# Queries and keys stacked side by side, three transfers a head, and a head's turn back one step sooner, in an attention and expert kernel

## What is computed

```python
q, k, v = (split_heads(x @ W + b) for W, b in ((Wq, bq), (Wk, bk), (Wv, bv)))
attn = q @ k.T / sqrt(32) - slopes * (Tx - 1 - arange(Tx))     # (4, 16, 512, 512)
p = softmax(where(causal, attn, min))
x = layernorm(x + (p @ v) @ Wo + bo)
probs = softmax(x @ Wr + br); top_w, e = top_k(probs, 1)
x = layernorm(x + top_w * (silu(x @ Wg[e]) * (x @ Wu[e])) @ Wd[e])
```

## Time and profile before

| what | us |
|---|---|
| median of 2 runs | 1335.26 (1333.82 to 1336.7) |
| the profiled execution | 1339.05 |
| its span (first to last instruction) | 1337.3 |
| PE busy | 1179.2 (88%) |
| DVE, ACT, POOL busy | 729.9, 592.3, 522.0 |
| first scores of the loop | at 29.2 |
| first products of the experts (L902) | at 614.4 |

### The profile page before, as it was taken

One profiled execution on the slowest core, in us unless ns is written; L12 is line 12 of the kernel. 1 busy time (PEld: TensorE's weight loads), 2 busy tenths in 40 slices (PEclk: granted clock), 3 DMA queues, 4 the chain that ended last, 5 costly groups with the idle time before them and its releaser, 6 DMA issues.

```text
span 1337.3 us, 25993 instructions
## 1 busy us (share of the span) xinstructions
PE 1179.2 (88%) x7658; PEld 1051.2 (79%) x7658; DVE 729.9 (55%) x1975; ACT 592.3 (44%) x1475; POOL 522.0 (39%) x662
## 2 busy tenths in 40 slices
PE   6867788888888887858999999999999999999994
PEld 5755676677667666647899889988999889998993
DVE  4544446544654456464655655465645664565565
ACT  3556666566566665723332323232322333233344
POOL 6744644454445454635311332133202331133136
PEclk9888988888888988767999999999999999999998
DMA  8222223222232222115322223231323122312302
GB/s 261 55 48 48 48 57 87 64 49 56 65 87 48 49 64 77 52 63 160 86 79 80 59 69 96 64 91 45 87 65 95 50 79 69 90 57 72 95 26 102
DMA packets 110336, 100.13 MB, mean 75 GB/s; under 512 B 13247, under 2 KB 82495, under 8 KB 110208
## 3 DMA queue, kind: packets, MB, share of 16 engines
q1 hardware_dynamic: 105440, 87.98, 23.8%
q0 software_dynamic: 3040, 9.18, 2.1%
q10 hardware_dynamic: 1728, 1.31, 0.3%
HBM read 64.74 MB, written 9.18 MB: 55 GB/s over the span
## 4 chain that ended last, share of the span: by engine, by line
PE 60%; SPq 9%; POOL 8%; DMA 7%; issue 6%; DVE 5%; ACT 5%; ACTq 0%; DVEq 0%; POOLq 0%
PE bank L902 33%; PE bank L674 9%; SPq L557 7%; POOL up_lo L1629 6%; PE bank L927 6%; DMA q_stack<-qk_lo 3%; PE bank L820 3%; DMA up_raw<-in_Wu_dram 3%; PE bank L914 2%; PE bank L780 2%; PE bank L795 2%; DVE bank L1283 1%; ACT up_hi L1057 1%; ACT qk_hi L983 1%; SPq L578 1%
## 5 line engine op out<-in xcount | busy, mean ns | idle before, releaser
L902 PE MATMUL bank<-up_hi,xsT_hi 128*128 x1216 | 356.2, 293 | 9.9 <-POOL up_lo L1629 9.4
L1629 POOL TENSOR_TENSOR up_lo<-up_raw,up_hi 128x256 fp32r<-128x256 f32 x241 | 171.7, 748 | 483.0 <-ACT up_hi L1057 482.8
L902 PE MATMUL bank<-up_hi,xsT_lo 128*128 x1216 | 344.6, 283 | 0.0
L902 PE MATMUL bank<-up_lo,xsT_hi 128*128 x1216 | 344.5, 283 | 0.0
L1620 POOL TENSOR_TENSOR pT_lo<-probs,pT_hi 128x512 fp32r<-128x512 f32 (+1 forms) x192 | 211.4, 1101 | 196.2 <-ACT pT_hi L1034 196.0
L1444 DVE SCALAR_TENSOR_TENSOR h_tok<-bank,row_weight,silu 128x128 f32<-128x128 f32 x304 | 93.4, 347 | 296.1 <-ACT silu L1138 296.1
L902 PEld LDWEIGHTS bank<-up_hi,xsT_hi 128*128 128x128 f32 x1216 | 233.3, 192 | 16.7 <-issue 16.4
L902 PEld LDWEIGHTS bank<-up_hi,xsT_lo 128*128 128x128 f32 x1216 | 234.0, 192 | 0.3
L902 PEld LDWEIGHTS bank<-up_lo,xsT_hi 128*128 128x128 f32 x1216 | 233.6, 192 | 0.0
L1138 ACT ACTIVATE silu<-bank 128x256 f32<-128x256 f32 (+1 forms) x160 | 59.9, 374 | 365.8 <-PE bank L902 365.8
L1461 DVE TENSOR_TENSOR y<-bank,y 128x512 f32<-128x512 f32 x295 | 199.0, 690 | 0.4
(11 more groups left out here) (181 smaller groups left out, 2145.5 us busy)
## 6 DMA issues: line engine op xcount, KB each, us to landing
up_raw<-in_Wg_dram SPq DMA_DIRECT2D x64, 256.0 KB, 3.5
up_raw<-in_Wu_dram SPq DMA_DIRECT2D x64, 256.0 KB, 4.5
down_raw<-in_Wd_dram SPq DMA_DIRECT2D x64, 256.0 KB, 2.6
k_stack<-qk_hi SPq DMA_DIRECT2D x128, 64.0 KB, 2.0
q_stack<-qk_hi SPq DMA_DIRECT2D x128, 64.0 KB, 2.0
x_tok<-in_x_dram SPq DMA_DIRECT2D x16, 256.0 KB, 3.8
k_stack<-qk_lo SPq DMA_DIRECT2D x64, 64.0 KB, 2.0
q_stack<-qk_lo SPq DMA_DIRECT2D x64, 64.0 KB, 2.0
```

The costliest lines, as they stand in the source:

```text
L902: mm = pe.matmul(bank[:, n * 2 * P:(n + 1) * 2 * P], a[:, s, k, :], up_w[w][k][:, :, :].rearrange("p a f -> p (a f)")[:, bass.ds(at, 2 * P ...
L1629: pool.tensor_tensor(up_w[1][k][:, e, :], up_raw[:, idx % NUPS, k, :, :].rearrange("p g f -> p (g f)"), up_w[0][k][:, e, :].bitcast(F32), ...
```

## The change

1. `qk_hi` and `qk_lo` become one buffer `qk` of four parts in the order low q, high q, high k, low k, and `q_stack` and `k_stack` become one buffer `stack` with both side by side in a slot. One transfer fills a third of the slot for both: three transfers a head with twice the bytes each (the first group keeps six a head, by `load_first_part`, since its keys are ready before its queries).
2. SP looks in every step, not only in every third, whether a head's stacks can be loaded.
3. On ACT the copy to `pvT` stands at the end of step s instead of early in step s+1; PE's turn stands in step s+1 instead of s+2; the copy of the high half, the sum and the division in step s+2 instead of s+3.
4. The plan takes the first job of its queue whose needs are met; rows' jobs are queued in other steps; V jobs of the first groups come later; K and Q of some groups come earlier in their group.

```diff
+LOW, HIGH = {WQ: 0, WK: 3}, {WQ: 1, WK: 2}
+STACKED = ((HIGH[WQ], HIGH[WK]), (LOW[WQ], HIGH[WK]), (HIGH[WQ], LOW[WK]))
...
-    row_steps = ((), (0, 1, 6), (0, 3), (2, 6)), ((), (0, 4), (0, 4), (0, 1, 5))
+    row_counts = (0, 3, 2, 2), (0, 2, 2, 3)
...
-                if any(k not in ready for k in needs(queue[0])):
+                now_job = next((j for j in queue if all(k in ready for k in needs(j))), None)
+                if now_job is None:
                     return
...
-                if m in (1, 2) and b < LAST:
+                if m == 2 and 0 < b < LAST:
                     queue.extend([("K", g + 1), ("Q", g + 1)])
...
-        if is_head_step(u, VL + PER_HEAD + 3):
-            ready.add(("o", (u - VL - PER_HEAD - 3) // PER_HEAD))
+        if is_head_step(u, VL + PER_HEAD + 2):
+            ready.add(("o", (u - VL - PER_HEAD - 2) // PER_HEAD))
...
-                for n in (WK, WQ):
-                    load_part(hd, n, False)
-                    load_part(hd, n, True)
+                for r, (q_part, k_part) in enumerate(STACKED):
+                    sp.dma_start(stack[r * HD:(r + 1) * HD, hd % NSTK, :, :].bitcast(F32),
+                                 qk[h * HD:(h + 1) * HD, q_part:k_part + 1:k_part - q_part, :].bitcast(F32)
+                                 ).then_inc(s_stack[hd % NSTK], 16)
...
                     load_row((u - ROW_AT) // PER_HEAD)
-                    for _ in range(2):
-                        if (next_stack < NB * NH and plan.flushed[("Q", next_stack // GH)] <= u
-                                and (next_stack < NSTK or (next_stack - NSTK) * PER_HEAD + PER_HEAD - 1 + LAG < u)):
-                            load_stacks(next_stack)
-                            next_stack += 1
+                for _ in range(2):
+                    if (next_stack < NB * NH and plan.flushed[("Q", next_stack // GH)] <= u
+                            and (next_stack < NSTK or (next_stack - NSTK) * PER_HEAD + PER_HEAD - 1 + LAG < u)):
+                        load_stacks(next_stack)
+                        next_stack += 1
...
-                if is_head_step(u, VL + PER_HEAD + 1):
-                    head_values((u - VL - PER_HEAD - 1) // PER_HEAD)
+                if is_head_step(u, VL + PER_HEAD):
+                    head_values((u - VL - PER_HEAD) // PER_HEAD)
...
-                if is_head_step(u, VL + PER_HEAD):
-                    head_copied((u - VL - PER_HEAD) // PER_HEAD)
-                if is_head_step(u, VL + PER_HEAD + 2):
-                    head_values((u - VL - PER_HEAD - 2) // PER_HEAD)
+                if is_head_step(u, VL + PER_HEAD + 1):
+                    head_values((u - VL - PER_HEAD - 1) // PER_HEAD)
                 if is_head_step(u, ROW_AT):
                     copy_row((u - ROW_AT) // PER_HEAD)
                 if LAG <= u < U + LAG:
                     unit_exp(u - LAG)
+                if is_head_step(u, VL + PER_HEAD - 1):
+                    head_copied((u - VL - PER_HEAD + 1) // PER_HEAD)
```

More of the change, by code:

```diff
@@ L165, in make_plan @@
         plan.flushed[job] = 0
-    ready = {("x", b, j) for b in range(2) for j in range(QT)} | {("read",) + job for job in first}
+    ready = {("begun", "OP", -1), ("begun", "logit", -1)} | {("x", b, j) for b in range(2) for j in range(QT)} | {("read",) + job for job in first}
     queue, left, now_job, pending, later = deque(), [], None, [], deque()
     rows_due, fresh = deque(), []
-    row_steps = ((), (0, 1, 6), (0, 3), (2, 6)), ((), (0, 4), (0, 4), (0, 1, 5))
+    row_counts = (0, 3, 2, 2), (0, 2, 2, 3)
     def needs(job):
@@ L178, in needs @@
         if kind == "OT":
-            return [("o", t // QT * NH + (DONE if t // QT == LAST else NH) - 1)]
-        return {"OP": [("read", "OT", t)], "x1t": [("ln", t)], "logit": [("read", "x1t", t)], "bv_wo": [("split", kind)]}[kind]
+            return [("o", t // QT * NH + (DONE if t // QT == LAST else NH) - 1), ("begun", "OP", t - 1)]
+        return {"OP": [("read", "OT", t)], "x1t": [("ln", t), ("begun", "logit", t - 1)], "logit": [("read", "x1t", t)], "bv_wo": [("split", kind)]}[kind]
     def flush(u):
@@ L202, in work @@
                     return
-                now_job = queue.popleft()
+                queue.remove(now_job)
+                ready.add(("begun",) + now_job)
                 plan.add(now_job, 2)
@@ L254, in make_plan @@
                 if g == 0:
-                    queue.extend([("K", 1), ("Q", 1), ("V", 1, 0), ("bv_wo", 0)])
+                    queue.extend([("K", 1), ("Q", 1), ("bv_wo", 0)])
                 elif m == 0:
                     queue.appendleft(("V", g // 2, 1))
-                elif m == 1:
-                    queue.append(("V", g // 2 + 1, 1))
-                elif m == GPB - 1 and b + 1 < NB:
+                    rows_due.extend((b - 1, n) for n in range(QT + 3))
+                elif g == 1:
+                    queue.append(("V", 1, 0))
+                elif m == 1 or g == 2:
+                    queue.appendleft(("V", b * GPB // 2 + 1, 1))
+                for _ in range(row_counts[b == LAST][m] if b else 0):
+                    queue.extend(row_jobs(*rows_due.popleft()))
+                if m == GPB - 1 and b + 1 < NB:
                     next_x = b + 1
                     queue.append(("V", (g + 1) // 2, 0))
-                if m == 0 and g:
-                    rows_due.extend((b - 1, n) for n in range(QT + 3))
             for j in range(QT):
@@ L391, in build @@
         xT_lo = p1.put("xT_lo", [P, KT, SEQ], F32R)
-        qk_hi = p1.put("qk_hi", [P, 2, SEQ], F32R)
-        qk_lo = p1.put("qk_lo", [P, 2, SEQ], F32R)
+        qk = p1.put("qk", [P, 4, SEQ], F32R)
         stacks_at = p1.at
-        k_stack = p1.put("k_stack", [3 * HD + 1, NSTK, SEQ], F32R)
-        q_stack = p1.put("q_stack", [3 * HD + 1, NSTK, SEQ], F32R)
+        stack = p1.put("stack", [3 * HD + 1, NSTK, 2, SEQ], F32R)
+        q_stack, k_stack = stack[:, :, 0, :], stack[:, :, 1, :]
         v = p1.put("v", [P, 2, QT, 2 * GH, VW], F32R)
@@ L548, in load_x, with load_first_part @@
                 sp.dma_start(x_tok[:, (b + 1) % 2, j, :], x_rows[b, :, j, :]).then_inc(s_x[b % 2][j], 16)
-            def load_part(hd, n, low):
-                h, slot = hd % GH, hd % NSTK
+            def load_first_part(h, n, low):
                 rows = slice(h * HD, (h + 1) * HD)
[L554 to L558, removed]
+                for r, (q_part, k_part) in enumerate(STACKED):
+                    part = k_part if n == WK else q_part
+                    if (part in LOW_PARTS) == low:
+                        sp.dma_start(stack[r * HD:(r + 1) * HD, h, 1 if n == WK else 0, :].bitcast(F32),
+                                     qk[rows, part, :].bitcast(F32)).then_inc(s_stack[h], 16)
             def load_first_stack(h, n, job):
                 sp.wait_ge(s_side_act, plan.act_number[job])
-                load_part(h, n, False)
+                load_first_part(h, n, False)
                 sp.wait_ge(s_side_dve, plan.number[job])
-                load_part(h, n, True)
+                load_first_part(h, n, True)
             def load_stacks(hd):
-                g = hd // GH
+                g, h = divmod(hd, GH)
                 sp.wait_ge(s_side_dve, max(done("K", g), done("Q", g)))
@@ L982, in take @@
                             act.wait_ge(s_stack[hd % NSTK], stack_count(hd))
-                    hi = act.activation(qk_hi[:, n, :], bank[:, :], ACT.Identity, bias=bias_col[:, n, m:m + 1])
+                    hi = act.activation(qk[:, HIGH[n], :], bank[:, :], ACT.Identity, bias=bias_col[:, n, m:m + 1])
                 elif kind == "V":
```

19 lines of the change are left out of this document (9 added, 10 removed).

## The result

The changed kernel takes 1289.97 us (median of 2 runs, 1287.9 to 1292.03) where the kernel before took 1335.26. The ratio is 0.9661, with a 95% interval of 0.9581 to 0.9741: 45 us or 3.4% faster. The forecast was 1258, so 32 us of the 77 that it promised are missing. The profiled execution has a span of 1290.2 us.

A forecast was written before the change was run, and what follows sets the result against it. PE bound the kernel (60% of the chain), with 60.7 us of stack waits and clock falls behind them; -56 - 29 - 4 + 9 + 5 - 2 = -77 from 1339.05 gave 1262, less 3.8 for the median 1258 us, range 1226 to 1292.

The forecast's parts named there:

- transfers sooner: Attention loop: SP issues stacks ahead of the row of maxima; PE's stack waits fall from 60 to 4 us, -56.
- clock back: Loop behind stack waits: 34 us lost at half clock return, less 5 for new falls in steps without side work, -29.
- a head's turn one step sooner: Loop: waits for pv_sum go, waits for pvT come; +9 us, the middle between -14 and +32.
- plan: Loop: eight more steps without side work, each leaving PE 0.57 us idle, +5 us.
- tail: Loop's end: the last head ends one step sooner, so the last output projections start sooner, -2 us.
- Rival D: Stack transfers: two pieces a partition double issue and flight, some 35 us of waits stay; about 1320; 0.10 with other reasons.
- rival A: Loop: short waits that are left make the clock fall about as often; 1287 us, chance 0.18.
- the sign of A: Loop: a mean clock under 0.90 would show that the clock keeps falling.
- The lower bound: Head's turn: the whole 13.6 us wait for pv_sum gone and nothing new, -14 us.
- The upper bound: Head's turn: 1.0 us later for each of 32 heads with keys or queries on the copy's step, +32 us.
- Rival B: Head's turn: PE waits for pvT uncovered in every head with a take, +32 instead of +9; 1281 us, chance 0.13.
- ACT's waits for copies: Loop: ACT's 19.9 us before qk_hi, mostly hidden; PE shows one wait of some 3 us on the maxima, -4.

The follow-up runs named there:

- e1: Kernel before with only the side-by-side stacks, three transfers a head, and SP's look in every step: 1258.57 us, ratio 0.9393.
- e2: Changed kernel with the head's copy, turn and sum put back in their steps of before: 1256.89 us, ratio 0.9391.
- e4: Changed kernel with the side-work plan of before; the sooner turn and new transfers stay: 1284.39 us, ratio 0.9596.
- e3: Changed kernel with PE's turn half a step later, behind the turned scores; ACT keeps its new order: 1266.49 us, ratio 0.9455.
- e8: Kernel before with only the head's copy, turn and sum one step sooner: 1345.22 us, ratio 1.0075.
- e5: Kernel before with only SP's look in every step, still six 64 KB transfers a head: 1285.03 us, ratio 0.9606.

## Why the prediction was right or wrong

| step | forecast, us | measured, us |
|---|---|---|
| transfers sooner | -56 | -55.5 of PE's idle time (before to e1), -56.4 (before to e2) |
| clock back | -29 | -24.5 of PE's busy time (before to e1), -26.6 (before to e2) |
| these two and ACT's waits | -89 | -77 by the medians, -80 in the traces |
| a head's turn one step sooner | +9 | +33 (e2 to after), +26 (e1 to e4) |
| plan | +5 | +5.6 with the turn sooner, -1.7 without |
| tail | -2 | +2.2 in the traces |

The forecast promised 77 us and the change gives 45. e2, the change without the sooner turn, has all the other terms: for it the forecast is -77 - 9 = -86, and it gave 79. So the turn, at +33 where I had +9, makes 24 of the 32 us that are missing, and all the rest about 7.

**Transfers: right.** I had left 4 us of stack waits; e1 has 3.2. I took 2.3 us of flight and it is 2.4. SP's first stack transfer comes 0.03 us behind the low part's end, and six issues take 3.92 us, 0.65 each where I took 0.63. Rival D is out: four of these six are in two pieces a partition, and neither SP nor the flight took twice as long.

**Clock: right in size, short by 2.4 us.** e2 has the new plan, whose eight more steps without side work I had charged with part of my 5 us, so it is the run to hold against -29; it gave 26.6. With the stack waits gone, and with the short waits for `pv_sum` still there, e1 and e2 run the loop at 0.94 and 0.95. So rival A is not what came from that. The Trainium skill, page "TensorE: Matmul & The Clock Gate", section "A second HAM failure mode: psum-queue depth-cycling", had spoken for it; in e1 the trace does not agree, since the loop's mean clock rose from 0.87 to 0.94 with 16 waits for `pv_sum` left, though it did not reach 1.00. In the changed kernel the clock is 0.92, between my 0.94 and the "under 0.90" that I had named as the sign of A, and e2 shows that the turn brings that part with this plan: the changed kernel comes out near A's 1287 by another way. That 1290 is still inside my range, which went up to 1292 for A's sake, is luck.

My reading of the earlier trace rows was loose: the 17 matmuls at full clock are a mix with 8-column ones, so that the counts 9 and 17 are not of like work. For one and the same operation the reading holds: behind a product of 512 columns (L674) the next matmul starts 0.43 us later at 0.50 (217.87 and 218.30) and 0.23 us later at 1.00 (219.00 and 219.23).

**The turn: the mechanism right, the size wrong.** The wait for `pvT` became PE's longest (42.6 us, for which I had given 10 to 40). I wrote that the turned scores of the stretch in the earlier trace rows would come 0.7 to 1.0 us later; they come 4.59 - 3.68 = 0.91 us later. I also wrote that ACT's other work covers the wait where PE has no side work, and there it does: that head is no longer than before. Where PE has side work a head lasts longer (6.54 us for 5.74, under e2). But then I took the middle between +32 and -14 and put +9 into the sum. That is the step that failed: the term was too small by 24 us, from both ends. The lower bound was no bound: I had just shown from the earlier trace rows that behind the wait for `pv_sum` PE would stand for the exponential all the same, so that -14 was worth about nothing. e3 shows it: there the waits for `pv_sum` are gone, and 16.7 us of other waits are new. The upper bound counted 32 heads, for keys and queries. With takes of every kind it is 44 heads in the new plan and 47 in the old one, at 0.63 us each as e1 and e4 have it. What I also left out is that the turn can cost clock: in e2 to after, 17.7 of 38 us are busy time, in e1 to e4 almost none. Rival B was this mechanism; I gave it 1281, and 0.13 where it deserved the first place. That e8 measured just 9 us is chance, since there late stacks hid the rest.

**ACT's waits for copies:** 19.9 us became 6.6, one wait. PE's waits for the maxima went from 5.7 to 4.1. What these are worth by themselves was not measured; it is inside e1.

**The plan: not told from nothing.** With the turn sooner it costs 5.6 by the medians, near my 5, but the intervals of e4 and after overlap (0.9555 to 0.9636, and 0.9581 to 0.9741), and without the turn it is -1.7. My eight steps at 0.57 us were an argument and no run shows them.

**The tail: the wrong way.** From the last scores to the experts' first products it is 568.6 - 497.7 = 70.9 us in after, and 614.2 - 545.5 = 68.7 before. The experts' part is as long as before (721.6 and 723.1 us), so nearly all of the difference lies in the loop, as forecast.

## What to carry to other kernels

The length of a wait is not what its removal brings: look in the timeline at what the engine would wait for next, and give the saving up to there only. Where an engine works in order, moving one of its steps sooner puts it ahead of work that is ready, and if the step's input is late, the engine stands for it; here it was enough to move the consumer back half a step (e3, 23 us), and no worse to undo the move (e2, 33 us). A wait that is seen in one place need not cost there: compare how long the same piece of work takes as a whole in both kernels, in many places. On a queue in order, small urgent messages stand behind bulk transfers: fewer, larger transfers are worth more for what they let through than for themselves (e5), and two late things hide each other's price, so measure each change both alone and beside the others (e8 against e2).

## What the runs showed of the hardware

A transfer's issue took SP little longer for 128 KB (0.65 us; six in 3.92, four of them in two pieces a partition) than for 64 KB in one piece (0.59), and inside the chip 128 KB landed in 2.4 us where 64 KB took 2.0. The 24 transfers of 64 KB that after keeps for its first group took 3.2 us. I had not expected that the clock would answer to a turn's waits with the one plan (0.95 to 0.92, e2 to after) and not with the other (0.94 to 0.96, e1 to e4); which waits make it fall here stays open.
